# Edge stage of a two-layer graph network: twelve transposes in one run on TensorE, both message casts ahead of both relus on ScalarE

## The chip, the cores and the metric

The kernel runs on one core of one Trainium2 chip. The metric is the time of one execution in microseconds, the median of several runs. PE is TensorE's matmul path and PEld its weight load, DVE is VectorE, ACT is ScalarE, POOL is GpSimd, SP is SyncE.

## The reference

Two graph layers with residuals and layer norms over 6250 nodes of 256 features and 100000 edges sorted by destination. The change lies in the first layer:

```
src, dst = edge_index
ei   = concat([x[src], edge_attr], axis=-1)          # 256 + 64 features
core = maximum(ei @ W1 + b1, 0.0) @ W2 + b2
gate = sigmoid(ei @ Wg + bg)
msg  = gate * core
agg  = segment_sum(msg, dst, num_segments=N)
out  = layernorm(agg + x) * gamma + beta
x    = layernorm(x + out)
```

The second layer (two hops of a normalised sum over edges, a product, a log softmax) follows and is not touched.

## The kernel before, in words

Setup. `x @ [W1 | Wg]` plus biases is computed once for each node and stored as `p_table` (6250 rows of 512 numbers). The rows of one edge's source then bring in the node part of both products at once, and only the 64 edge features are left to multiply.

Edge stage. The edges are worked through in 196 groups of 512 (4 tiles of 128). Each engine has its own list of stages written out group by group; `at_group(stage, i, s, lag)` calls a stage for group G + lag in step G. Semaphores alone tie the engines together. For a group g:

- POOL, `gather` (L801): four indirect DMAs bring the rows of `p_table` into `gathered`, which has two places (g even or odd). It waits until `hidden_product` and `gate_seeded` of group g - 2 are done. Ahead of it POOL does `lower_msg` (L822) of the first half of the messages of group g - 4.
- ScalarE and VectorE split the edge features into an upper part and a remainder (`round_ea` L1285, `lower_ea` L1779). PE's `turn_ea` (L939) transposes them, four transposes into bank 7, and `copy_ea` (L1291) brings them back as `ea_turned_sb`, signalled by `ea_ready`.
- PE, `hidden_product`: for each of two banks k (0 and 1) the products of `w_e_hi` and `w_e_lo` with `ea_turned_sb`, 512 columns each (L950, L951), then four transposes of the gathered rows added on top (L953). Each bank has to be free first: `hidden_ready` of the group before.
- ScalarE, `upper_hidden(k)` (L1299): the relu of bank k into `hidden_hi`; VectorE, `lower_hidden(k)` (L1786): the remainder `hidden_lo`, which frees the bank.
- PE, `gate_product` (L963, L964): eight matmuls of 256 columns onto banks 2 and 3, which ScalarE has seeded with the gathered gate part (`seed_gate` L1329); `open_gate` (L1320) takes the sigmoid.
- PE, `core_product` (L976): 24 matmuls of 256 columns (three products of split factors for each of 4 tiles and 2 halves of the features) onto banks 4 and 5, seeded with the bias by `seed_core` (L1313).
- VectorE, `message` (L1796): gate times core for each half of the group, into `room`. ScalarE, `upper_msg(half)` (L1306): the upper part `msg_hi`. The remainder of half 0 is POOL's (L822), of half 1 VectorE's `lower_msg` (L1802).
- PE, `scatter` (L990, L992): eight matmuls of a one-hot matrix with both parts of the messages into bank 6. VectorE's `add_window` (L1828) adds the bank to `agg`; in a middle stretch of the stage once for two groups, else once for each group.

In step G, PE does the core product of G, the hidden and gate products of G + 2, the scatter of G - 1 and the edge features' transposes of G + 4, in this order. VectorE and ScalarE also work on finished chunks of 7 node blocks between their stages: VectorE in small pieces, ScalarE with the scaling of rows (L1336, L1343) and, once for each of the four EARLY chunks (EARLY = NC - 3), a cast of a whole chunk (L1383) just ahead of `copy_ea`.

Hops. After the edge stage come two hops over the graph and the last stage. They share no code with the change.

Of the kernel before, what the change touches and what calls it, by code (L numbers as in the profile page):

```python
# [8 lines left out]
P = 128  # L9
GROUP = 512  # L10
TILES = 4
# [39 lines left out]
def wait_count(engine, semaphore, count):  # L51

    if not isinstance(count, int) or count > 0:
        engine.wait_ge(semaphore, count)
# [131 lines left out]
def gnn_kernel(nc, x, src, dst, edge_attr, W1, b1, W2, b2, Wg, bg, gamma, beta, Wl, bl, out):  # L186
    N, H = x.shape
    E, DE = edge_attr.shape
    KC = H // P
# [35 lines left out]
    with ExitStack() as ctx:  # L225
        def sb(name, shape, dt=F32):
            return ctx.enter_context(nc.sbuf_tensor(name, shape, dt))

        def sem(name):
            return ctx.enter_context(nc.semaphore(name))  # L230

        banks = ctx.enter_context(nc.psum_tensor("banks", [P, 8, 512], F32))
# [5 lines left out]
        def at(name, offset, shape, dt=F32):  # L238

            return nc.alloc_sbuf_tensor_at(name, shape, dt, offset=arena_at + offset).ap()  # L240
# [4 lines left out]
        w_e_hi = at("w_e_hi", EDGE_AT, [P, H2], F32R)  # L245
        w_e_lo = at("w_e_lo", EDGE_AT + 2048, [P, H2], F32R)
# [5 lines left out]
        ea_turned_sb = at("ea_turned_sb", EDGE_AT + 14336, [P, 2, GROUP], F32R)  # L252
# [66 lines left out]
        ident = sb("ident", [P, P])  # L319
# [48 lines left out]
        gathered = sb("gathered", [P, 2, TILES, H2])  # L368
# [33 lines left out]
        S = {n: sem(n) for n in names}  # L402
# [23 lines left out]
        def over_groups(engine, step, first, last):  # L426

            for g in range(first, 2):
                step(g // 2, g % 2)
            with engine.Fori(1, R - 3) as i:  # L430
                for s in range(2):
                    step(i, s)
            for g in range(NG - 6, last):
                step(g // 2, g % 2)

        def msg_of(table, s, half):

            return table[:, TILES * s + 2 * half:TILES * s + 2 * half + 2, 0:H]

        def at_group(stage, i, s, lag):  # L440

            turn, slot = i + (s + lag) // 2, (s + lag) % 2
            if not isinstance(turn, int) or 0 <= 2 * turn + slot < NG:
                stage(turn, slot, 2 * turn + slot)
# [397 lines left out]
        def _(pe):  # L842
# [87 lines left out]
            for bank in range(2, 6):  # L930
                last = nc.tensor.matmul(banks[:, bank, :], ident[:, :], bias_in[:, :], start=True, stop=True)
# [8 lines left out]
                                               ea_split[:, s, j, :, :].bitcast(F32).rearrange("p b d -> p (b d)"), ident[:, :])  # L940
                last.then_inc(S["ea_turned"], 1)

            def hidden_product(turn, s, g):

                pe.wait_ge(S["ea_ready"], g + 1)
                pe.wait_ge(S[f"p_gathered{s}"], 16 * TILES * (turn + 1))
                for k in range(KC):
                    columns = slice(k * P, (k + 1) * P)
                    wait_count(pe, S["hidden_ready"], 2 * g + k - 1)
                    nc.tensor.matmul(banks[:, k, :], w_e_hi[:, columns], ea_turned_sb[:, s, :], start=True, stop=False)  # L950
                    nc.tensor.matmul(banks[:, k, :], w_e_lo[:, columns], ea_turned_sb[:, s, :], start=False, stop=False)  # L951
                    for j in range(TILES):
                        last = nc.tensor.matmul(banks[:, k, j * P:(j + 1) * P], gathered[:, s, j, columns], ident[:, :],  # L953
                                                start=False, stop=j == TILES - 1, is_transpose=True)
                    last.then_inc(S["hidden_product"], 1)

            def gate_product(turn, s, g):
# [56 lines left out]
            def edge_steps(scatter_stage, looped):  # L1014
                def step(i, s):
                    at_group(core_product, i, s, 0)
                    at_group(hidden_product, i, s, 2)
                    at_group(gate_product, i, s, 2)
                    at_group(scatter_stage, i, s, -1)
                    at_group(turn_ea, i, s, 4)  # L1020
                if looped:
                    over_groups(pe, step, -5, NG + 1)
                else:
                    for g in range(-5, NG + 1):
                        step(g // 2, g % 2)
# [217 lines left out]
        def _(act):  # L1243
# [49 lines left out]
            def upper_hidden(k):  # L1293

                def stage(turn, s, g):
                    if k == 0:
                        wait_count(act, S["core_done"], 2 * (g - 1))
                    act.wait_ge(S["hidden_product"], 2 * g + k + 1)
                    nc.scalar.activation(hidden_hi[s][k], banks[:, k, :], ACT.Relu).then_inc(S["hidden_upper"], 1)  # L1299
                return stage  # L1300

            def upper_msg(half):

                def stage(turn, s, g):
                    act.wait_ge(S["msg_ready"], 2 * g + half + 1)
                    nc.scalar.copy(msg_of(msg_hi, s, half), msg_of(msg, s, half)).then_inc(S["msg_upper"], 1)  # L1306
                return stage
# [46 lines left out]
            def node_rows_at(g):  # L1354

                for c in range(NC - 2):
                    j = g - begins[c + 1]
                    if 0 <= j < CHUNK:
                        normed_row(c, j)
                    if 1 <= j <= CHUNK:  # L1360
                        scaled_row(c, j - 1)

            def step(i, s, in_order=True):
                at_group(copy_ea, i, s, 3)
                at_group(round_ea, i, s, 5)
                if in_order and isinstance(i, int):
                    node_rows_at(2 * i + s)
                at_group(seed_gate, i, s, 2)
                at_group(upper_msg(0), i, s, 0)
                at_group(upper_hidden(0), i, s, 2)  # L1370
                at_group(upper_msg(1), i, s, 0)
                at_group(upper_hidden(1), i, s, 2)
                at_group(seed_core, i, s, 1)
                at_group(open_gate, i, s, 2)
# [110 lines left out]
            with act.If(in_order):  # L1485
                for g in range(-5, NG):
                    if g in upper_at:
                        upper_rows(upper_at.index(g))
                    step(g // 2, g % 2)
                upper_rows(EARLY)  # L1490
                for c in range(EARLY + 1, NC):
                    node_rows(c)
                    upper_rows(c)
                hops()
            with act.Else():
                over_groups(act, lambda i, s: step(i, s, False), -5, NG)
                act.wait_ge(S["agg_added"], NG)
                for c in range(NC):
                    node_rows(c)
                for c in range(NC):  # L1500
                    upper_rows(c)
                hops()
# [819 lines left out]
```

## Time and profile before

| | us |
|---|---|
| runs | 2490.89 (median), 2490.82, 2492.63 |
| profiled execution, span of the core | 2488.3 |
| PE busy in the span | 2315.5 |
| VectorE, ScalarE, POOL busy | 1927.1, 1651.3, 1641.2 |
| mean granted TensorE clock | 0.971 |

The profile is of one further execution. For it the profile gives the span, from its first to its last instruction, and no other time; the run times also hold what lies around the span. Lines of the order of time read: start in us from the span's start, duration in us, engine, line, operation, output and inputs, how many instructions were merged, and in brackets the engine's idle time before and what ended it. Matmul ends are modelled, so the next start may come before the end that is shown.

### The profile page before, as it was taken

What the parts mean: (1) busy time and instruction counts of PE and PEld (TensorE: products, weight loads), DVE (VectorE), ACT (ScalarE), POOL (GpSimd) and SP (SyncE); (2) the same over time, 40 slices, a digit from 0 to 9 for tenths busy, and PEclk for the clock granted to TensorE, in tenths of its full rate; (3) what the DMA queues carried; (4) which work ended last, traced back from release to release, by engine and by line L of the source; (5) the groups of instructions that cost most, each with busy time, mean ns of one, the idle gap of its engine ahead of it and who ended that gap; (6) DMA issues with size and microseconds to landing.
All of it is one profiled execution on the core that took longest, in us unless ns stands there. A gap on an engine that the chain in (4) does not pass through costs nothing. (4 is left out here: it accounts for less than half of the span.)

```text
span 2488.3 us, 48732 instructions
## 1 busy us (share of the span) xinstructions
PE 2315.5 (93%) x16053; PEld 1833.1 (74%) x16053; DVE 1927.1 (77%) x4467; ACT 1651.3 (66%) x3119; POOL 1641.2 (66%) x1581
## 2 busy tenths in 40 slices
PE   7889999999999999999999996689999999999973
PEld 3369999999999999999999995145555554555542
DVE  6748878888887877888888989998888874447673
ACT  1158888888888889889998996454577751013232
POOL 0177777777777777777777773355676763777773
PEclk9989999999999999999999998799999999999996
DMA  6465656655556556656666662345556635776652
GB/s 220 163 211 169 170 168 173 172 171 169 168 170 169 170 168 188 179 171 186 183 186 183 183 186 84 99 123 135 149 153 162 181 88 178 263 238 211 211 163 79
DMA packets 276158, 422.41 MB, mean 170 GB/s; under 512 B 127618, under 2 KB 198548, under 8 KB 273860
## 3 DMA queue, kind: packets, MB, share of 16 engines
q0 software_dynamic: 90368, 281.11, 39.3%
q1 hardware_dynamic: 170028, 116.99, 15.4%
q10 hardware_dynamic: 15512, 21.17, 2.5%
q8 instruction: 134, 2.20, 0.4%
q14 instruction: 116, 0.95, 0.1%
HBM read 354.78 MB, written 64.37 MB: 168 GB/s over the span
## 5 line engine op out<-in xcount | busy, mean ns | idle before, releaser
L801 POOL DMA_INDIRECT gathered<-p_table,src_t x784 | 773.4, 987 | 275.6 <-issue 196.8
L801 POOL DMA_INDIRECT gathered<-hop_table,src_t x576 | 584.0, 1014 | 336.0 <-issue 154.5
L976 PE MATMUL banks<-w_hi,hidden_hi 128*128 128x256 f32 x1568 | 458.3, 292 | 3.9 <-ACT banks L1313 3.8
L976 PE MATMUL banks<-w_lo,hidden_hi 128*128 128x256 f32 x1568 | 441.8, 282 | 0.0
L976 PE MATMUL banks<-w_hi,hidden_lo 128*128 128x256 f32 x1568 | 441.2, 281 | 0.0
L1426 ACT CAST counts<-banks 128x686 f32 (+3 forms) x382 | 295.8, 774 | 155.6 <-PE banks L1038 76.4
L1796 DVE TENSOR_TENSOR room<-banks,gate 128x512 f32<-128x512 f32 x392 | 265.3, 686 | 76.5 <-PE banks L976 75.8
L822 POOL TENSOR_TENSOR msg_lo<-room,msg_hi 128x512 fp32r<-128x512 f32 x196 | 250.7, 1279 | 93.4 <-ACT msg_hi L1306 92.3
L1299 ACT ACTIVATE hidden_hi<-banks 128x512 fp32r<-128x512 f32 x392 | 235.0, 600 | 114.2 <-PE banks L953 111.5
L976 PEld LDWEIGHTS banks<-w_hi,hidden_hi 128*128 128x128 f32 x1568 | 297.3, 190 | 5.9 <-issue 4.2
L976 PEld LDWEIGHTS banks<-w_lo,hidden_hi 128*128 128x128 f32 x1568 | 298.3, 190 | 0.0
L976 PEld LDWEIGHTS banks<-w_hi,hidden_lo 128*128 128x128 f32 x1568 | 297.6, 190 | 0.0
L1038 PE MATMUL banks<-codes,low_hot 128*128 128x343 f16 (+3 forms) x958 | 239.6, 332 | 57.9 <-DVE codes L2010 52.8
L1786 DVE SCALAR_TENSOR_TENSOR hidden_lo<-banks,hidden_hi 128x512 fp32r<-128x512 f32 x392 | 263.1, 684 | 37.7 <-ACT hidden_hi L1299 29.7
L1064 PE MATMUL banks<-parts,counts 128*128 128x512 f16 x980 | 286.7, 379 | 0.0
L1306 ACT CAST msg_hi<-room 128x512 fp32r<-128x512 f32 x392 | 242.5, 619 | 48.6 <-DVE room L1796 39.6
L1106 PE MATMUL banks<-gathered,hot_half 128*128 128x256 f16 x1152 | 221.7, 284 | 44.3 <-DMA gathered<-hop_table,src_t 40.0
L1106 PEld LDWEIGHTS banks<-gathered,hot_half 128*128 128x128 f16 x1152 | 113.8, 101 | 170.9 <-DMA gathered<-hop_table,src_t 48.7
L953 PE MATMUL banks<-ident,gathered 128*128 128x128 f32 x1568 | 235.5, 273 | 0.0
L953 PEld LDWEIGHTS banks<-ident,gathered 128*128 128x128 f32 x1568 | 196.5, 141 | 51.9 <-issue 0.4
L1329 ACT COPY banks<-gathered 128x512 f32<-128x512 f32 x392 | 223.8, 623 | 3.6 <-DMA gathered<-p_table,src_t 3.6
L2010 DVE TENSOR_SCALAR codes<-wide,code_c 128x686 f16<-128x686 f16 (+3 forms) x551 | 220.8, 401 | 0.0
(224 smaller groups left out, 5304.3 us busy)
## 6 DMA issues: line engine op xcount, KB each, us to landing
ea<-in_edge_attr SPq DMA_DIRECT2D x196, 128.0 KB
counts_saved<-counts SPq DMA_DIRECT2D x16, 1568.0 KB, 9.7
ring<-counts_saved SPq DMA_DIRECT2D x16, 1568.0 KB, 7.6
gathered<-p_table,src_t POOLq DMA_INDIRECT x784
p_table<-p_t ACTq DMA_DIRECT2D x48, 256.0 KB, 2.6
hop_table<-parts SPq DMA_DIRECT2D x12, 896.0 KB
gathered<-hop_table,src_t POOLq DMA_INDIRECT x576, 2.9
x_saved<-x_room SPq DMA_DIRECT2D x7, 896.0 KB, 6.1
```

What stands on the lines that cost most here:

```text
L801: pool.indirect_dma_start(out=rows[:, n % slots, j, :], out_offset=None, in_=table[:, :], in_offset=bass.IndirectOffsetOnAxis(ap=src_t[:, ...
L822: nc.gpsimd.tensor_tensor(msg_of(msg_lo, g % 2, 0), msg_of(msg, g % 2, 0), msg_of(msg_hi, g % 2, 0).bitcast(F32), ALU.subtract).then_inc(S ...
L953: last = nc.tensor.matmul(banks[:, k, j * P:(j + 1) * P], gathered[:, s, j, columns], ident[:, :], start=False, stop=j == TILES - 1, is_tr ...
L976: last = nc.tensor.matmul(banks[:, 4 + half, j % 2 * H:(j % 2 + 1) * H], lhs, rhs, start=False, stop=n == len(products) - 1, skip_group_ch ...
L1038: last = nc.tensor.matmul(banks[:, bank, 0:each], low[:, :], code[:, each * n:each * (n + 1)], start=opens, stop=closes and (n > 0 or not ...
L1064: last = nc.tensor.matmul(banks[:, 4 + m % 2, 0:H2], counts[:, b, P * (m % BLOCKS):P * (m % BLOCKS + 1)], parts[:, b, :], start=b == 0, st ...
L1106: last = nc.tensor.matmul(banks[:, bank_of_turn(k, turn), 0:H], hot_half[:, turn % HOT_TURNS * TILES + j, :], hop_rows[:, turn % HOP_SLOTS ...
L1299: nc.scalar.activation(hidden_hi[s][k], banks[:, k, :], ACT.Relu).then_inc(S["hidden_upper"], 1)
L1306: nc.scalar.copy(msg_of(msg_hi, s, half), msg_of(msg, s, half)).then_inc(S["msg_upper"], 1)
L1426: nc.scalar.copy(in_blocks_of(e, coming.pop(0) + shared, width - shared), product_of(e, int(shared))).then_inc(S["evac_done"], 1)
L1786: nc.vector.scalar_tensor_tensor(out=hidden_lo[s][k], in0=banks[:, k, :], scalar=0.0, in1=hidden_hi[s][k].bitcast(F32), op0=ALU.max, op1=A ...
L1796: nc.vector.tensor_tensor(msg_of(msg, s, half), banks[:, 4 + half, :].rearrange("p (j n) -> p j n", j=2), gate[s][:, 2 * half:2 * half + 2 ...
```

## The change

On PE the eight transposes of the gathered rows leave `hidden_product` and become a stage of their own, `turn_rows`, which opens both banks. In the step, `turn_ea` moves from the end to behind the core product, with `turn_rows` behind it. The 512-column products are then added onto the transposed rows. On ScalarE `upper_msg(1)` moves ahead of `upper_hidden(0)`.

```diff
-            def hidden_product(turn, s, g):
-
-                pe.wait_ge(S["ea_ready"], g + 1)
+            def turn_rows(turn, s, g):
+
                 pe.wait_ge(S[f"p_gathered{s}"], 16 * TILES * (turn + 1))
                 for k in range(KC):
                     columns = slice(k * P, (k + 1) * P)
                     wait_count(pe, S["hidden_ready"], 2 * g + k - 1)
-                    nc.tensor.matmul(banks[:, k, :], w_e_hi[:, columns], ea_turned_sb[:, s, :], start=True, stop=False)
-                    nc.tensor.matmul(banks[:, k, :], w_e_lo[:, columns], ea_turned_sb[:, s, :], start=False, stop=False)
                     for j in range(TILES):
-                        last = nc.tensor.matmul(banks[:, k, j * P:(j + 1) * P], gathered[:, s, j, columns], ident[:, :],
-                                                start=False, stop=j == TILES - 1, is_transpose=True)
+                        nc.tensor.matmul(banks[:, k, j * P:(j + 1) * P], gathered[:, s, j, columns], ident[:, :],
+                                         start=j == 0, stop=False, is_transpose=True, skip_group_check=True)
+
+            def hidden_product(turn, s, g):
+
+                pe.wait_ge(S["ea_ready"], g + 1)
+                for k in range(KC):
+                    columns = slice(k * P, (k + 1) * P)
+                    nc.tensor.matmul(banks[:, k, :], w_e_hi[:, columns], ea_turned_sb[:, s, :], start=False, stop=False,
+                                     skip_group_check=True)
+                    last = nc.tensor.matmul(banks[:, k, :], w_e_lo[:, columns], ea_turned_sb[:, s, :], start=False, stop=True,
+                                            skip_group_check=True)
                     last.then_inc(S["hidden_product"], 1)
...
             def edge_steps(scatter_stage, looped):
                 def step(i, s):
                     at_group(core_product, i, s, 0)
+                    at_group(turn_ea, i, s, 4)
+                    at_group(turn_rows, i, s, 2)
                     at_group(hidden_product, i, s, 2)
                     at_group(gate_product, i, s, 2)
                     at_group(scatter_stage, i, s, -1)
-                    at_group(turn_ea, i, s, 4)
...
                 at_group(seed_gate, i, s, 2)
                 at_group(upper_msg(0), i, s, 0)
+                at_group(upper_msg(1), i, s, 0)
                 at_group(upper_hidden(0), i, s, 2)
-                at_group(upper_msg(1), i, s, 0)
                 at_group(upper_hidden(1), i, s, 2)
```

The order on PE from the last matmul of a core product to the first of the gate product, before. L950 and L951 are the 512-column products, L953 the transposes of gathered rows:

```order
L976 MATMUL banks<-w_hi,hidden_lo_66 128x256
L950 MATMUL banks<-ea_turned_sb,w_e_hi 128x512 [waits hidden_ready,p_gathered0,ea_ready]
L951 MATMUL banks<-ea_turned_sb,w_e_lo 128x512
L953 MATMUL banks<-ident,gathered 128x128 x4
L950 MATMUL banks<-ea_turned_sb,w_e_hi 128x512 [waits hidden_ready]
L951 MATMUL banks<-ea_turned_sb,w_e_lo 128x512
L953 MATMUL banks<-ident,gathered 128x128 x4
L963 MATMUL banks<-w_e_hi,ea_turned_sb 128x256 [waits gate_seeded]
```

A third run of four transposes (L939) stands at the end of the step, ahead of the next core product.

The same place after the change. L983 is the core product, L950 now the transposes of gathered rows, L958 and L960 the 512-column products:

```order
L983 MATMUL banks<-w_hi,hidden_lo_66 128x256
L939 MATMUL banks<-ident,ea_split 128x128 [waits ea_ready,ea_split]
L939 MATMUL banks<-ident,ea_split 128x128 x3
L950 MATMUL banks<-ident,gathered 128x128 [waits hidden_ready,p_gathered0]
L950 MATMUL banks<-ident,gathered 128x128 x3
L950 MATMUL banks<-ident,gathered 128x128 [waits hidden_ready]
L950 MATMUL banks<-ident,gathered 128x128 x3
L958 MATMUL banks<-ea_turned_sb,w_e_hi 128x512 [waits ea_ready]
L960 MATMUL banks<-ea_turned_sb,w_e_lo 128x512
L958 MATMUL banks<-ea_turned_sb,w_e_hi 128x512
L960 MATMUL banks<-ea_turned_sb,w_e_lo 128x512
L970 MATMUL banks<-w_e_hi,ea_turned_sb 128x256 [waits gate_seeded]
```

All twelve transposes of a step now stand between the core product and the first 512-column product, and the next core product follows the scatter.

The order on ScalarE from the gate's seeding to the gate's sigmoid, before:

```order
L1329 COPY banks<-gathered 128x512 [waits gate_ready]
L1306 CAST msg_hi<-room 128x2x256 [waits msg_ready]
L1299 ACTIVATE hidden_hi_63<-banks 128x512 [waits hidden_product,core_done]
L1306 CAST msg_hi<-room 128x2x256 [waits msg_ready]
L1299 ACTIVATE hidden_hi_64<-banks 128x512 [waits hidden_product]
L1313 COPY banks<-bias_core 128x512 [waits msg_ready] x2
L1320 ACTIVATE gate_59<-banks 128x512 [waits msg_ready,gate_product] x2
```

And after the change:

```order
L1337 COPY banks<-gathered 128x512 [waits gate_ready]
L1314 CAST msg_hi<-room 128x2x256 [waits msg_ready] x2
L1307 ACTIVATE hidden_hi_61<-banks 128x512 [waits hidden_product,core_done]
L1307 ACTIVATE hidden_hi_62<-banks 128x512 [waits hidden_product]
L1321 COPY banks<-bias_core 128x512 [waits msg_ready] x2
```

The second cast of the messages (L1306, now L1314) went from between the relus (L1299, now L1307) to ahead of both.

## Rows read from the trace of the kernel before

**Rows 1.** The page: span, and busy time of each engine.

```profile
span 2488.3 us, 48732 instructions
...
PE 2315.5 (93%) x16053; PEld 1833.1 (74%) x16053; DVE 1927.1 (77%) x4467; ACT 1651.3 (66%) x3119; POOL 1641.2 (66%) x1581
```

**Rows 2.** Windows, first to last core product: length, busy (count) by engine, PEclk, DMA.

```profile
163.75:1529.54 1365.79, 1362.30 (x10881) 1309.51 (x10881) 1136.00 (x2081) 1206.18 (x2405) 1010.07 (x967) 1.00 0.61 174
```

**Rows 3.** Waits of PE in the edge stage: us in total, times, longest.

```profile
PE banks L976 <- ACT banks L1313: 3.8, 6, 1.2
```

**Rows 4.** Order of time on PE in one group.

```profile
600.03 0.40 PE L950 MATMUL banks<-ea_turned_sb,w_e_hi 128*128 128x512 f32 x1
...
600.50 0.60 PE L953 MATMUL banks<-ident,gathered 128*128 128x128 f32 x4
...
600.83 0.27 PE L953 MATMUL banks<-ident,gathered 128*128 128x128 f32 x1
600.85 0.48 PE L950 MATMUL banks<-ea_turned_sb,w_e_hi 128*128 128x512 f32 x1
601.17 0.39 PE L951 MATMUL banks<-ea_turned_sb,w_e_lo 128*128 128x512 f32 x1
601.40 0.60 PE L953 MATMUL banks<-ident,gathered 128*128 128x128 f32 x4
...
603.61 0.28 PE L992 MATMUL banks<-msg_lo,hot_window 128*128 128x256 f32 x1
...
604.09 0.36 PE L976 MATMUL banks<-w_hi,hidden_hi 128*128 128x256 f32 x1
```

**Rows 5.** Groups by line and form, edge stage, PE: busy us, mean ns, idle before.

```profile
L950 PE MATMUL banks<-ea_turned_sb,w_e_hi 128*128 128x512 f32 x388 | 169.0, 435 | 0.0
L951 PE MATMUL banks<-ea_turned_sb,w_e_lo 128*128 128x512 f32 x388 | 152.7, 393 | 0.0
```

**Rows 6.** Order of time on PE in the setup, transposes of L852 and L907.

```profile
45.76 0.38 PE L852 MATMUL banks<-ident,agg 128*128 128x128 f32 x2
45.98 0.60 PE L907 MATMUL banks<-ident,gathered 128*128 128x128 f32 x4
46.41 1.88 PE L860 MATMUL banks<-room,x_turned_sb 128*128 128x512 f32 x4
```

**Rows 7.** Order of time on ScalarE in the same group as rows 4.

```profile
601.19 0.60 ACT L1299 ACTIVATE hidden_hi<-banks 128x512 fp32r<-128x512 f32 x1 [0.90 <-PE banks L953]
...
602.69 1.11 ACT L1313 COPY banks<-bias_core 128x512 f32<-128x512 f32 x2
...
604.69 0.60 ACT L1291 CAST ea_turned_sb<-banks 128x512 fp32r<-128x512 f32 x1
```

**Rows 8.** Order of time in a group that waits, on ScalarE and PE.

```profile
1017.67 1.72 ACT L1383 ACTIVATE parts<-agg 128x1792 f16<-128x1792 f32 x1
...
1023.67 1.11 ACT L1313 COPY banks<-bias_core 128x512 f32<-128x512 f32 x2
...
1024.42 0.36 PE L976 MATMUL banks<-w_hi,hidden_hi 128*128 128x256 f32 x1
```

**Rows 9.** Order of time on VectorE in the same group as rows 4.

```profile
600.23 0.69 DVE L1796 TENSOR_TENSOR room<-banks,gate 128x512 f32<-128x512 f32 x1 [0.59 <-PE banks L976]
...
604.06 0.48 DVE L1828 SCALAR_TENSOR_TENSOR agg<-banks,first_row,agg 128x257 f32 x1 [0.54 <-PE banks L992]
...
605.97 0.68 DVE L1796 TENSOR_TENSOR room<-banks,gate 128x512 f32<-128x512 f32 x1
```

**Rows 10.** Order of time on POOL in the same group as rows 4.

```profile
602.27 0.96 POOL L801 DMA_INDIRECT gathered<-p_table,src_t  x1 [0.70 <-PE banks L953]
```

**Rows 11.** Setup and start of the edge stage: windows view, and PE in order of time.

```profile
29.00:41.00 12.00, 12.00 (x66) 7.75 (x65) 7.14 (x12) 1.49 (x4) 0.00 (x0) 1.00 0.71 256
...
150.00:158.00 8.00, 4.47 (x17) 3.91 (x18) 1.17 (x3) 2.81 (x7) 4.28 (x6) 0.50 0.78 244
...
154.52 1.05 PE L953 MATMUL banks<-ident,gathered 128*128 128x128 f32 x4
```

## Prediction

> **What bounds the kernel now.** I read the page first, then the windows view over the edge stage, then the order of time on each engine inside one group. The page says a span of 2488.3 us in which PE is busy 93% and nothing else over 77% [rows 1]. The change touches only the edge stage. Its 196 groups of 512 edges run from the first core product at 163.75 to the last at 1529.54: 1365.79 us for 195 steps, 7.00 us each, with PE busy 1362.30 of it at a clock of 1.00 [rows 2]. PE's waits in this stage are one line, 3.8 us in 6 waits [rows 3]. So the stage costs what PE's instruction stream costs. Another order on ScalarE can give back at most these 3.8 us; all else must come out of PE's own spacing. In the order of time on PE the reader should look at the starts, since ends are modelled: 512-column matmuls start 0.23 us apart, and a run of four transposes stands between the others three times in a group [rows 4].
>
> **PE: twelve transposes in one run.** No instruction is added or removed: per group still 12 transposes, 4 matmuls of 512 columns and 40 of 256 or 258. What changes is how often a run of transposes ends: three times before, once after.
> A tempting row is the first matmul behind a run: L950 at 600.85 shows 0.48 us, where L951 shows 0.39 [rows 4]. Over the stage L950 has a mean of 435 ns against L951's 393; only every second L950 stands behind a run, so that is 84 ns a run [rows 5]. Taken as a fee for the switch, two switches fewer would save 2 x 0.084 x 196 = 33 us.
> I don't take it so. Count from start to start: the first run begins at 600.50, the second matmul behind it at 601.17. Take off one 512-column matmul (0.23, 601.17 to 601.40): four transposes cost 0.44, 0.11 each [rows 4]. The matmul behind the run is booked as started only 0.02 us after the last transpose (600.83 and 600.85) and pays the rest of that transpose's 0.11 inside its own longer row. The 84 ns are the missing part of the last transpose, not something on top of it. A longer run in the setup says the same: six transposes from 45.76 to 46.41, 0.65 us, again 0.11 each [rows 6]. A run of n costs n x 0.11 from start to start, whatever n is; twelve in one run cost what 3 x 4 do. By the rows a transpose streams 128 columns and still takes nearly as long as a product of 256, (7.00 - 12 x 0.11 - 4 x 0.23)/40 = 0.12; what both have in common is a new load of weights ahead of each.
> The Trainium skill has the reason, in "TensorE: Matmul & The Clock Gate", section "LDWEIGHTS (loading the stationary operand)": a load takes its columns over 1.2 in ns, 107 ns for 128 columns, whatever the matmuls around it are. By that rule twelve transposes take 12 x 107 ns in one run or in three, and nothing is saved; with the 84 ns as a fee it would be 33 us. It speaks against a gain here.
> Bounds: the rows are good to 0.01 us, so two ends of a run fewer are worth between 0 and 2 x 0.01 x 196 = 3.9 us. I take **-1 us**, since 0.44 for a run is nearer to 4 x 0.11 than to anything 0.01 above it.
>
> **PE's new order, and who waits.** Let 0 be the end of the core product, where L950 starts (600.03). Before, the first relu starts at 601.19, +1.16, 0.09 after the modelled end of its bank's last transpose (600.83 and four in 0.60 from 600.50, 601.10) [rows 4, 7]. In the change the 12 transposes take 1.31, the two 512-column matmuls of the first bank start at +1.31 and +1.54, and the second ends at 1.54 + 0.39 = +1.93, so the relu can start at +2.02. The second bank is ready 0.46 later. ScalarE's instructions follow each other in 0.50 (relu, cast, relu from 601.19 to 602.69), so the second relu starts at about +2.52 and seed_core at +3.02, where it stood at +2.66 [rows 7]. What does PE need? In a group that waits, seed_core started at 1023.67 and the core product at 1024.42, 0.75 later [rows 8]. The next core product is due at 604.09, +4.06 [rows 4], so seed_core may start as late as +3.31. Margin 0.65 before, **0.29 after**: no wait in a plain group. ScalarE also has the room, busy 1206.18/195 = 6.19 of 7.00 us [rows 2]. The rest, edit by edit:
> - turn_ea now stands right behind the core product. Its ea_ready comes from L1291, which starts at 604.69 and takes 0.60; 0.36 later it ends at 605.65 and is wanted at 607.03. Margin 1.4 [rows 7].
> - upper_msg(1) ahead of upper_hidden(0): its message starts at 600.23, +0.20, and takes 0.69, so the cast runs from about +0.96 to +1.58, in time in which ScalarE stood idle (0.90 before the relu) [rows 7, 9]. It costs nothing; it would be paid in full if the message came 0.45 later.
> - The scatter now closes the group: its last matmul moves from 603.61, +3.58, to about +4.01. VectorE's add_window started 0.45 after it and starts 0.43 later; behind it stand lower_msg, lower_ea and the first message, which goes from 605.97 to 606.40 and ends at 607.1. The second message is due at 607.23 [rows 4, 9]. Hidden, with 0.1 to spare; late next is that second message, wherever node work lies between.
> - POOL: the gather waits for hidden_product, and starts at 602.7 in place of 602.27 [rows 10]; lower_msg also moves back by 0.4. POOL is busy 1010.07/195 = 5.2 of 7.00 us [rows 2], the loop closes, and the rows land 0.4 later, for a product two groups on.
> - turn_rows waits for hidden_ready of the group before; VectorE's hidden_lo of it is done half a group earlier. Nothing.
>
> **Groups that wait.** PE's 3.8 us of waits lie in few groups [rows 3]. In four (one for each of the EARLY chunks) ScalarE has a 1.72 us cast of node rows, and everything behind it is late; there seed_core, not PE, sets the step [rows 8]. In some others VectorE's node work does it. After, two things are added there: the second cast must wait for a message that comes 0.6 behind the first, where ScalarE would go on after 0.5, +0.10; and ScalarE enters the group 0.36 later. In the four that is 4 x 0.46 = 1.8 us. In the others 0.1 to 0.5 each, 1 us together. In the last thirty groups a window is added in every group, not every second, and VectorE has no room for the 0.43: a few new waits, 0 to 2 us, I take 0.5. Together **+3.3 us**, bounds 0 (ScalarE's unbroken pairs take it all back) and +8 (twice as many groups wait).
>
> **Sum.** -1 + 3.3 = +2.3 us on the profiled span of 2488.3. The median of the three runs is 2490.89, 2.6 above that span, which is what lies around it; so 2490.9 + 2.3 = **2493 us**.
>
> **Rivals.**
> A. The 84 ns are a real fee. For: the longer rows [rows 4, 5]. Against: start-to-start times and the run of six [rows 4, 6]. Time: 2490.9 - 33 + 2.3 = 2460. Chance 0.07.
> B. ScalarE's chain becomes the bound, and it is slower: hidden_product, relu, relu, seed_core, core product, in every group. It decides when the first relu starts more than 0.29 us behind my +2.02. For: the margin halves, and no row of before shows a relu behind a 512-column matmul. Against: the relu's 0.09 behind the modelled end, and ScalarE's 6.19 of 7.00. With the relu 0.35 late it is 0.06 x 190 = 11 us, 2504; with 0.5 late 40 us, 2533. Chance 0.12, half of it near the lower figure.
> C. The clock. Twelve transposes in a row are 1.3 us with few columns streamed. If the granted clock fell to 1.2 GHz in that stretch, the row at a clock of 0.50 prices it: four transposes 1.05 us against 0.60 [rows 4, 11]; 12 would lose 1.35 us a group, 265 us in all, 2755. Against: a stretch of 12 us in the setup in which runs of 10 and 18 transposes alternate with four products each holds 1.00 [rows 11]. Chance 0.02.
> D. The reordering works and the new waits don't come: 2490, inside the forecast's range. That it does not do what it says is excluded: in the order one run of twelve stands in place of three, and both casts ahead of the relus.
>
> **How the numbers follow.** Forecast 0.79, A 0.07, B 0.12, C 0.02. A measurement of this kernel tells about 0.2% from no change, 5 us: the band is 2485.9 to 2495.9. The forecast's own bounds are 2490.9 - 3.9 = 2487 and 2490.9 + 8 = 2499; what lies above the band is 0.05 of chance. Slower: 0.05 + 0.11 of B + 0.02 = 0.18. Faster: A and a hundredth beside it, 0.08. Same: 0.74. The range is 2487 to 2501: A, C and the dearer part of B are left out, the cheapest part of B is in.
>
> **What would show it.** Twelve transposes starting 0.11 apart, then 512-column matmuls from +1.31; plain steps of 6.99 to 7.00 us; the first relu at +2.0 and seed_core at +3.0; PE waiting 5 to 8 us in all for seed_core in place of 3.8; the clock at 1.00 throughout. I am wrong if a plain step is 6.84 (A), if it is over 7.02 with PE waiting for seed_core in every group (B), or if another wait (ea_ready, hidden_ready) shows there.

## The result, and the profile after

The changed kernel takes 2495.36 us (median of 14 runs, 2493.0 to 2497.92), the kernel before 2490.32 us beside it (14 runs, 2488.6 to 2494.08). The ratio is 1.002, with a 95% interval of 1.0012 to 1.0027: 5 us slower, just at the 0.2% that the prediction named as the edge of what can be told. The forecast was 2493 in a range of 2487 to 2501. The profiled execution has a span of 2492.8 us, 4.5 more than before.

The page of the changed kernel, span and busy time by engine, against [rows 1]:

```profile
span 2492.8 us, 48731 instructions
...
PE 2315.2 (93%) x16053; PEld 1851.6 (74%) x16053; DVE 1941.9 (78%) x4467; ACT 1665.5 (67%) x3119; POOL 1629.8 (65%) x1581
```

PE's work is the same. VectorE and ScalarE show 15 and 14 us more for the same instructions; of VectorE's, 14 us lie in one instruction (the one-hot, L1809 before and L1817 now, a mean of 1.12 us before and 1.20 after), of which the last section tells.

The windows view from the first to the last core product, against [rows 2], with the same columns:

```profile
164.79:1534.50 1369.71, 1363.98 (x10880) 1327.96 (x10881) 1150.12 (x2081) 1220.78 (x2405) 1000.60 (x966) 1.00 0.60 173
```

The stage takes 1369.71 us, 3.92 more. What comes behind it takes 958.3 us in place of 958.8. The clock is 1.00 as before, so rival C is out for the stage.

The waits of PE in that stage, against [rows 3]:

```profile
PE banks L983 <- ACT banks L1321: 5.0, 7, 1.3
PE banks L939 <- ACT ea_turned_sb L1299: 0.7, 4, 0.2
```

The first line is seed_core, 5.0 in place of 3.8 us. The second is new: turn_ea waits for the edge features' copy in four groups.

The order of time on PE in one group, from the end of the core product to the first gate matmul, against [rows 4]:

```profile
601.51 0.28 PE L983 MATMUL banks<-w_hi,hidden_lo 128*128 128x256 f32 x1
601.63 0.60 PE L939 MATMUL banks<-ident,ea_split 128*128 128x128 f32 x4
602.07 1.04 PE L950 MATMUL banks<-ident,gathered 128*128 128x128 f32 x8
602.86 0.48 PE L958 MATMUL banks<-ea_turned_sb,w_e_hi 128*128 128x512 f32 x1
603.17 0.39 PE L960 MATMUL banks<-ea_turned_sb,w_e_lo 128*128 128x512 f32 x1
603.40 0.40 PE L958 MATMUL banks<-ea_turned_sb,w_e_hi 128*128 128x512 f32 x1
603.64 0.39 PE L960 MATMUL banks<-ea_turned_sb,w_e_lo 128*128 128x512 f32 x1
603.87 0.28 PE L970 MATMUL banks<-w_e_hi,ea_turned_sb 128*128 128x256 f32 x1
```

From 601.63 to 603.17, less one 512-column matmul of 0.23, the twelve transposes take 1.31 us, 12 x 0.109. Only behind the last transpose is there a long 512-column row, 0.48. The other long rows are gone, and nothing was won by it: where a matmul was booked 0.02 us behind the last transpose of a run, the next transpose now starts a full 0.11 behind it.

ScalarE in the same group, against [rows 7]:

```profile
601.63 0.62 ACT L1314 CAST msg_hi<-room 128x512 fp32r<-128x512 f32 x1
602.56 0.62 ACT L1314 CAST msg_hi<-room 128x512 fp32r<-128x512 f32 x1 [0.31 <-DVE room L1804]
603.66 1.09 ACT L1307 ACTIVATE hidden_hi<-banks 128x512 fp32r<-128x512 f32 x2 [0.49 <-PE banks L960]
604.64 1.11 ACT L1321 COPY banks<-bias_core 128x512 f32<-128x512 f32 x2
```

With 601.63 as 0 the relus start at +2.03 and seed_core at +3.01; the prediction had +2.02 and +3.02. VectorE's add_window (606.10) is at +4.47, predicted +4.46.

The plain step is read best over 100 groups. Before, and after the change, starts of core products:

```profile
303.09 0.36 PE L976 MATMUL banks<-w_hi,hidden_hi 128*128 128x256 f32 x1
...
1003.09 0.36 PE L976 MATMUL banks<-w_hi,hidden_hi 128*128 128x256 f32 x1
```

```profile
304.63 0.28 PE L983 MATMUL banks<-w_hi,hidden_hi 128*128 128x256 f32 x1
...
1004.96 0.28 PE L983 MATMUL banks<-w_hi,hidden_hi 128*128 128x256 f32 x1
```

100 steps take 700.00 us before and 700.33 after: 3 ns a step more, 0.6 us over the stage.

The start-up, on PE, before: idle times over 0.2 us from the first transposes of edge features to the first core product.

```profile
146.45 1.12 PE L939 MATMUL banks<-ident,ea_split 128*128 128x128 f32 x4 [4.34 <-DVE ea_split L1779]
148.33 1.09 PE L939 MATMUL banks<-ident,ea_split 128*128 128x128 f32 x4 [0.77 <-ACT ea_turned_sb L1291]
153.53 0.77 PE L950 MATMUL banks<-ea_turned_sb,w_e_hi 128*128 128x512 f32 x1 [4.11 <-DMA gathered<-p_table,src_t]
...
163.75 0.36 PE L976 MATMUL banks<-w_hi,hidden_hi 128*128 128x256 f32 x1 [0.42 <-ACT banks L1313]
```

And after:

```profile
145.19 1.12 PE L939 MATMUL banks<-ident,ea_split 128*128 128x128 f32 x4 [4.61 <-DVE ea_split L1787]
...
152.13 1.97 PE L950 MATMUL banks<-ident,gathered 128*128 128x128 f32 x8 [2.12 <-DMA gathered<-p_table,src_t]
159.47 0.73 PE L939 MATMUL banks<-ident,ea_split 128*128 128x128 f32 x4 [2.37 <-ACT ea_turned_sb L1299]
164.79 0.36 PE L983 MATMUL banks<-w_hi,hidden_hi 128*128 128x256 f32 x1 [0.32 <-ACT banks L1321]
```

From the first transposes to the first core product it was 163.75 - 146.45 = 17.30 us and is now 164.79 - 145.19 = 19.60, 2.3 us more. PE stands 2.37 us at turn_ea, waiting for ScalarE's copy, with eight transposes and the hidden product of another group behind it in the queue. Before, turn_ea was the last stage of a step and nothing was behind it but the next step. ScalarE starts that copy only at 158.73, behind this step's relus (which wait for PE's hidden product), a table load of 1.28 us and the sigmoids.

The wait is only part of the loss. While PE stood there the granted clock was 1.00 (157 to 159 us); once it went on it fell to 0.50, that is 1.2 GHz (160 to 163.1 us). The windows view from turn_ea to the first gate matmul, with the columns of [rows 2]:

```profile
159.47:163.36 3.89, 3.89 (x17) 3.56 (x17) 0.42 (x1) 1.72 (x4) 1.12 (x2) 0.56 0.73 222
```

The same twelve transposes and four products take 603.87 - 601.63 = 2.24 us in the plain group shown above. Against that, the slow clock costs 1.65 us here. The kernel before works at 0.50 up to 159 us and at 1.00 from 160 us on; the changed one was at 1.00 by 157 us and lost it again. How the 2.3 us divide between wait and clock, these two profiles don't tell.

In this profile the setup ahead of the first transposes was 1.3 us shorter, which hides half of the loss. The granted clock goes with it: between 105 and 115 us it is 1.00 in the profile of the changed kernel and 0.83 in the one before. It stays at 1.00 in the profiles of five of the six kernels here that have turn_ea moved forward, and in none of the eight others; but e8 and f8 are the same kernel and have 0.83 and 1.00. Whether this is chance is open.

The long steps: in the group with the first whole-chunk cast, against [rows 8], after the change:

```profile
1019.83 1.72 ACT L1391 ACTIVATE parts<-agg 128x1792 f16<-128x1792 f32 x1
...
1022.16 0.63 PE L939 MATMUL banks<-ident,ea_split 128*128 128x128 f32 x4 [0.17 <-ACT ea_turned_sb L1299]
...
1025.90 1.11 ACT L1321 COPY banks<-bias_core 128x512 f32<-128x512 f32 x2
...
1026.64 0.36 PE L983 MATMUL banks<-w_hi,hidden_hi 128*128 128x256 f32 x1
```

That step takes 7.68 us (7.33 before). The four steps with a cast are 7.68, 7.61, 7.61, 7.37 (before 7.33, 7.26, 7.26, 7.00). From the start of the cast to seed_core it is 6.07 us, before 6.00; the rest of the 0.35 is that ScalarE enters the group later. Over all steps longer than 7.035 us, the first two left out, the excess above 7.00 sums to 6.0 us, before to 3.1.

So, of the profiled pair: start-up +2.3, long steps +2.9, plain steps +0.6, less 1.3 ahead of the stage and 0.5 behind it; the first two steps (13.78 us, before 13.33) make up the rest to 4.5. The runs tell which parts are real.

### The profile page after: what moved, and what is told of

Same layout as the page of the kernel before. It is cut to its first block and busy times, and to the rows that moved or that the text cites. A ratio compares the mean times of both kernels' runs of the same rounds, so it can differ in the third digit from the quotient of the medians.

```text
span 2492.8 us, 48731 instructions
## 1 busy us (share of the span) xinstructions
PE 2315.2 (93%) x16053; PEld 1851.6 (74%) x16053; DVE 1941.9 (78%) x4467; ACT 1665.5 (67%) x3119; POOL 1629.8 (65%) x1581
## 5 line engine op out<-in xcount | busy, mean ns | idle before, releaser
L801 POOL DMA_INDIRECT gathered<-p_table,src_t x784 | 762.4, 972 | 284.2 <-issue 193.8
L983 PE MATMUL banks<-w_hi,hidden_hi 128*128 128x256 f32 x1568 | 442.8, 282 | 5.4 <-ACT banks L1321 5.0
L983 PE MATMUL banks<-w_lo,hidden_hi 128*128 128x256 f32 x1568 | 442.8, 282 | 0.0
L983 PE MATMUL banks<-w_hi,hidden_lo 128*128 128x256 f32 x1568 | 442.1, 282 | 0.0
L1794 DVE SCALAR_TENSOR_TENSOR hidden_lo<-banks,hidden_hi 128x512 fp32r<-128x512 f32 x392 | 252.2, 684 | 86.9 <-ACT hidden_hi L1307 85.6
L822 POOL TENSOR_TENSOR msg_lo<-room,msg_hi 128x512 fp32r<-128x512 f32 x196 | 252.3, 1287 | 98.0 <-ACT msg_hi L1314 97.4
L983 PEld LDWEIGHTS banks<-w_hi,hidden_hi 128*128 128x128 f32 x1568 | 297.2, 190 | 7.4 <-issue 3.6
L983 PEld LDWEIGHTS banks<-w_hi,hidden_lo 128*128 128x128 f32 x1568 | 298.5, 190 | 0.0
L983 PEld LDWEIGHTS banks<-w_lo,hidden_hi 128*128 128x128 f32 x1568 | 297.5, 190 | 0.0
L1314 ACT CAST msg_hi<-room 128x512 fp32r<-128x512 f32 x392 | 240.2, 625 | 80.6 <-DVE room L1804 71.8
L1307 ACT ACTIVATE hidden_hi<-banks 128x512 fp32r<-128x512 f32 x392 | 213.2, 596 | 75.2 <-PE banks L960 74.1
L1817 DVE TENSOR_TENSOR hot_window<-iota,lo_t 128x512 fp32r<-128x512 f32 x196 | 234.3, 1195 | 0.0
L1321 ACT COPY banks<-bias_core 128x512 f32<-128x512 f32 x392 | 218.4, 601 | 0.0
```

The lines of the kernel that those rows point to most:

```text
L801: pool.indirect_dma_start(out=rows[:, n % slots, j, :], out_offset=None, in_=table[:, :], in_offset=bass.IndirectOffsetOnAxis(ap=src_t[:, ...
L822: nc.gpsimd.tensor_tensor(msg_of(msg_lo, g % 2, 0), msg_of(msg, g % 2, 0), msg_of(msg_hi, g % 2, 0).bitcast(F32), ALU.subtract).then_inc(S ...
L983: last = nc.tensor.matmul(banks[:, 4 + half, j % 2 * H:(j % 2 + 1) * H], lhs, rhs, start=False, stop=n == len(products) - 1, skip_group_ch ...
L1794: nc.vector.scalar_tensor_tensor(out=hidden_lo[s][k], in0=banks[:, k, :], scalar=0.0, in1=hidden_hi[s][k].bitcast(F32), op0=ALU.max, op1=A ...
L1817: nc.vector.tensor_tensor(hot_window[:, TILES * s:TILES * (s + 1), :], iota[:, :].unsqueeze(1).to_broadcast([P, TILES, P]), columns.unsque ...
```

## The experiments

Twelve runs in four sets, each compared with the kernel before on the same chip.

**e1_pe_only.** TensorE's part alone.

```diff
                 at_group(upper_msg(0), i, s, 0)
-                at_group(upper_msg(1), i, s, 0)
                 at_group(upper_hidden(0), i, s, 2)
+                at_group(upper_msg(1), i, s, 0)
                 at_group(upper_hidden(1), i, s, 2)
```

(against the changed kernel)

> TensorE's part of the change alone, ScalarE's order as before (the second message cast stands between the relus again). My theory (weight loads set the pace of the transposes, and what PE loses it loses to late seeds): the first relu starts at +1.97 as in the change, the cast and the second relu follow in steps of 0.50, so seed_core starts at about +3.44, 0.13 behind the +3.31 that PE needs. A plain step is 7.10 to 7.14 us and the kernel takes 2515 to 2525 us. Rival (ScalarE's reordering is what costs the 5 us, PE's part is free): 2490 to 2492 us, plain step 7.00.

Measured: 2534.68 us, ratio 1.0177 (1.0161 to 1.0192). ScalarE and PE, in order of time:

```profile
601.52 0.60 ACT L1307 ACTIVATE hidden_hi<-banks 128x512 fp32r<-128x512 f32 x1 [1.04 <-PE banks L960]
602.01 0.61 ACT L1314 CAST msg_hi<-room 128x512 fp32r<-128x512 f32 x1
602.52 0.60 ACT L1307 ACTIVATE hidden_hi<-banks 128x512 fp32r<-128x512 f32 x1
603.01 1.11 ACT L1321 COPY banks<-bias_core 128x512 f32<-128x512 f32 x2
...
603.75 0.35 PE L983 MATMUL banks<-w_hi,hidden_hi 128*128 128x256 f32 x1
```

seed_core is at 603.01, the core product 0.74 later, and the plain step is 7.21 us. The rival (ScalarE's order is what costs) is out; without ScalarE's part TensorE's costs 44 us. My figure was low: it added the 0.50 of one cast to a seed_core at +2.94, where the changed kernel's stands at +3.01. The relu at +2.03 and three intervals of together 1.49 give +3.52, 0.21 behind the prediction's limit of +3.31, and 0.21 x 195 = 41 of the 44 us. It is rival B of the prediction, made real by one cast of 0.5 us (the prediction had priced a delay of 0.5 at 40 us), and it shows that the margin was in truth 0.3 us.

**e2_act_only.** ScalarE's part alone, on the kernel before (the same two lines, the other way).

> ScalarE's part alone, TensorE's order as before. My theory: both banks' relus have room, seed_core starts 0.05 to 0.1 earlier, PE's plain step stays 7.00 and the waits stay 3 to 5 us in all: 2489 to 2492 us. Rival (the second cast ahead of the first relu delays the chain by itself): 2494 to 2496 us, as in the change.

Measured: 2491.32 us, ratio 1.0 (0.9991 to 1.0009). ScalarE's order costs nothing by itself and brings nothing by itself: PE waits for seed_core 4.5 us in the profile, plain step 7.00. In the trace, though, two of the long steps, the one three groups behind the first cast and the last but two, are 7.86 and 7.72 us as in the changed kernel (7.87 and 7.69; before 7.63 and 7.37). So about 0.6 of the changed kernel's 2.9 us in long steps come from ScalarE's order alone.

**e3_ea_last.** The whole change, with turn_ea left at the end of the step.

```diff
                     at_group(core_product, i, s, 0)
-                    at_group(turn_ea, i, s, 4)
                     at_group(turn_rows, i, s, 2)
...
                     at_group(scatter_stage, i, s, -1)
+                    at_group(turn_ea, i, s, 4)
```

> The whole change except that turn_ea stays at the end of the step: eight transposes in one run behind the core product, four ahead of the next. My theory: the wait of turn_ea for ea_ready goes, the relus come 0.44 earlier (first at +1.53), seed_core at about +2.5, and the long steps shrink to those of before: 2489 to 2492 us, plain step 7.00. Rival A (a fee of 0.084 us for each run of transposes left): one run more than in the change would make it 16 us slower than the change, 2511 us. Rival 2 (opening the banks with transposes costs PE something): 2494 to 2496 us.

Measured: 2492.62 us, ratio 1.0008 (0.9999 to 1.0017). The start-up is back at 17.0 us:

```profile
148.89 1.12 PE L939 MATMUL banks<-ident,ea_split 128*128 128x128 f32 x4 [4.34 <-DVE ea_split L1787]
...
155.76 1.97 PE L950 MATMUL banks<-ident,gathered 128*128 128x128 f32 x8 [3.90 <-DMA gathered<-p_table,src_t]
165.90 0.36 PE L983 MATMUL banks<-w_hi,hidden_hi 128*128 128x256 f32 x1 [0.41 <-ACT banks L1321]
```

In the stage no wait for ea_turned_sb is left, the first two steps take 13.27 us (13.33 before), and the steps with the first three casts are 7.33, 7.31 and 7.31 in place of 7.68, 7.61 and 7.61. The profile has one odd step of 7.72, where PE waited 0.49 us for gathered rows. With one run of transposes more than the changed kernel it is not 16 us slower but 3 us faster. The 0.6 us past my upper figure of 2492 is a plain step that alternates between 6.99 and 7.02; why it does I did not try to find.

**e5_more_runs.** The kernel before with the same twelve transposes in eight runs in place of three.

```diff
                     nc.tensor.matmul(banks[:, k, :], w_e_hi[:, columns], ea_turned_sb[:, s, :], start=True, stop=False)
-                    nc.tensor.matmul(banks[:, k, :], w_e_lo[:, columns], ea_turned_sb[:, s, :], start=False, stop=False)
                     for j in range(TILES):
+                        if j == 2:
+                            nc.tensor.matmul(banks[:, k, :], w_e_lo[:, columns], ea_turned_sb[:, s, :], start=False, stop=False)
...
+                    if g + 5 < NG:
+                        turn_one(g + 5, j)
...
-                    at_group(turn_ea, i, s, 4)
+                    if looped or 2 * i + s < 1:
+                        at_group(turn_ea, i, s, 4)
```

(turn_one is one of turn_ea's four transposes, behind each tile of the scatter)

> The kernel before, with the same twelve transposes of a group in eight runs in place of three: 2 + 2 in each of the two banks around the second 512-column matmul, and the four of the edge features one by one between the scatter's matmuls. Theory (a transpose costs its own or the next weight load, 0.109 us, wherever it stands): plain step 7.00 to 7.02 us, 2489 to 2494 us. Rival A (leaving a run costs 0.084 us): 5 x 0.084 x 196 = 82 us more, 2572 us, plain step 7.42.

Measured: 2494.2 us, ratio 1.0013 (1.0004 to 1.0023); the plain step is 7.026 us, both just above what my theory had. The scatter with single transposes between, on PE:

```profile
604.69 0.28 PE L1003 MATMUL banks<-msg_lo,hot_window 128*128 128x256 f32 x1
604.81 0.27 PE L939 MATMUL banks<-ident,ea_split 128*128 128x128 f32 x1
604.84 0.36 PE L1001 MATMUL banks<-msg_hi,hot_window 128*128 128x258 f32 x1
605.04 0.28 PE L1003 MATMUL banks<-msg_lo,hot_window 128*128 128x256 f32 x1
605.16 0.27 PE L939 MATMUL banks<-ident,ea_split 128*128 128x128 f32 x1
```

Each lone transpose has its long row behind it (0.36 against 0.28) and yet costs 0.11: from 604.81 to 605.16 are a transpose and two matmuls, 0.35 = 0.11 + 2 x 0.12. Five more runs cost 0.026 us a step, 5 ns each, where a fee of 84 ns would have made 0.42 us and 82 us in all. Rival A is out. The reason, that the next load of weights sets the pace, agrees with all of this, and no run varied the load alone.

**e4_cast_spread, e8_rows_first, e9_both_cures, e6_before_spread.** These four ran together, on a chip where the kernel before took 2648.76 us.

> The whole change, and the four casts of a chunk of node rows (1.72 us each on ScalarE, ahead of copy_ea) cut into pieces of two blocks, one piece a group, ahead of the relus. Theory (about half of the 5 us is four groups in which the cast makes everything late, 0.6 us each after the change against 0.3 before): the long steps at the casts go, PE's waits for seed_core fall, 2492.5 to 2494 us, start-up as in the change. Rival (the cost is in every plain group, or in noise of the start): 2495 to 2497 us.

> The whole change with turn_rows ahead of turn_ea in the run of twelve. Theory (in the start-up PE waits 2.4 us at turn_ea for ea_ready, with eight transposes behind it that it could have done): from the first transposes to the first core product 19.6 us become 17.9 to 18.7, the rest stays, 2494 to 2495 us. Rival (the start-up is only the gather's chance from run to run): 19.6 us stays or varies with no relation to the order, 2495 to 2496 us.

> The whole change with turn_ea back at the end of the step and the four casts cut into pieces. Theory (the loss is start-up plus late groups, and nothing is in the transposes' order itself): 2490 to 2492 us, no difference from the kernel before that can be told; start-up 17.0 to 17.4 us; no step over 7.3 us in the middle of the stage. Rival (opening the banks with transposes costs by itself): 2493 us or more.

> The kernel before with the four casts cut into pieces, nothing else. Theory: the three or four steps of 7.3 us go, 1 us in all, 2489 to 2491 us, which can hardly be told from before. Rival (the pieces delay more groups than the whole cast did, since each costs its own start): 2492 us or more.

Measured: e4 2716.37 us (ratio 1.0258, 1.0231 to 1.0286), e8 2689.87 (1.0155, 1.0127 to 1.0182), e9 2681.9 (1.0128, 1.0099 to 1.0156), e6 2677.39 (1.0102, 1.007 to 1.0134). None of these answers its question. On this chip VectorE and ScalarE stop together for about 2 us in many groups, while PE and POOL go on, as here in e6 (VectorE, then ScalarE):

```profile
477.12 0.68 DVE L1811 TENSOR_TENSOR room<-banks,gate 128x512 f32<-128x512 f32 x1
479.95 0.69 DVE L1811 TENSOR_TENSOR room<-banks,gate 128x512 f32<-128x512 f32 x1 [2.15 <-remote]
```

```profile
477.84 0.62 ACT L1306 CAST msg_hi<-room 128x512 fp32r<-128x512 f32 x1
480.09 0.60 ACT L1299 ACTIVATE hidden_hi<-banks 128x512 fp32r<-128x512 f32 x1 [1.63 <-PE banks L953]
```

The profile names no cause within the core. All that can be read is that the change's order with turn_ea in front (e8) loses 1.5% there and 0.2% elsewhere; that it is the smaller margin that tells is a guess. Three of the four had a fault of mine besides: the edit moved VectorE's work on the chunk by two groups as well (`lower_at = [g + 4 ...]`), SP's store of the chunk waited for it, and the loads of edge features stood behind the store. In e6 ScalarE waited for them in 6 places:

```profile
ACT ea_split L1285 <- DMA ea<-in_edge_attr: 35.2, 6, 8.6
```

The four were run again on other chips, with the fault removed.

**f8_rows_first.** The whole change, turn_rows ahead of turn_ea.

```diff
                     at_group(core_product, i, s, 0)
-                    at_group(turn_ea, i, s, 4)
                     at_group(turn_rows, i, s, 2)
+                    at_group(turn_ea, i, s, 4)
                     at_group(hidden_product, i, s, 2)
```

> The same kernel as e8 again (the whole change with turn_rows ahead of turn_ea), on another chip, since the chip of the second call ran the kernel before in 2649 us. Theory as there: start-up from the first transposes to the first core product 17.9 to 18.7 us in place of 19.6, time 2494 to 2495 us. Rival: 19.6 us, 2495 to 2496 us.

Measured: 2494.72 us, ratio 1.0021 (1.0012 to 1.003). The start-up is 163.58 - 145.59 = 17.99 us, and the wait for the copy 1.58 us in place of 2.37:

```profile
145.59 1.12 PE L939 MATMUL banks<-ident,ea_split 128*128 128x128 f32 x4 [4.56 <-DVE ea_split L1787]
...
160.73 0.63 PE L939 MATMUL banks<-ident,ea_split 128*128 128x128 f32 x4 [1.58 <-ACT ea_turned_sb L1299]
163.58 0.36 PE L983 MATMUL banks<-w_hi,hidden_hi 128*128 128x256 f32 x1 [0.35 <-ACT banks L1321]
```

The trace shows the start-up cured by 1.6 us. Most of it is the clock. PE stood 1.58 us in place of 2.37, and from there to the first core product the granted clock is 1.00:

```profile
160.73:163.58 2.85, 2.50 (x17) 2.15 (x17) 1.52 (x3) 2.85 (x7) 2.06 (x3) 1.00 0.73 214
```

The changed kernel takes 164.79 - 159.47 = 5.32 us from the end of its wait to the core product: of the 2.47 us more, 1.65 are the slow clock and the other 0.82 the eight transposes that f8 has ahead of the wait. The copy itself came 0.8 us later, counted from the first gathered rows. No run varied PE's idle time alone. The first two steps take 13.78 us as in the changed kernel; moving turn_ea behind turn_rows does not cure them. Nor does it change the cast groups: there PE no longer waits for the copy, and the four steps are still 7.68, 7.61, 7.61 and 7.35. In the time the cure can't be seen: the interval covers both readings, so this rests on the trace alone. The stage itself (1369.77 us) is that of the change.

**f4_cast_pieces.** The whole change, each of the four casts in four pieces over two groups.

```diff
+                if known:
+                    piece_at(2 * i + s, 0)
                 at_group(upper_msg(1), i, s, 0)
+                if known:
+                    piece_at(2 * i + s, 1)
                 at_group(upper_hidden(0), i, s, 2)
...
-                    if g in upper_at:
-                        upper_rows(upper_at.index(g))
```

(piece_at casts two blocks of the chunk, in the two groups from upper_at on)

> The whole change with each of the four whole-chunk casts cut into four pieces over two groups, one ahead of each of the places where ScalarE is idle, and VectorE's part and the stores left at their old groups (in e4 they had moved by two groups, and the edge features' loads queued behind the stores). Theory: the four steps of 7.6 us go, 2492.5 to 2494 us; ScalarE never waits over 2 us for the edge features. Rival (the long steps come from VectorE's node work alone): 2495 to 2496 us, steps of 7.6 stay.

Measured: 2494.42 us, ratio 1.0014 (1.0005 to 1.0023). The step at the first cast went from 7.68 to 7.05, with one of 7.33 behind it, and the others from 7.61, 7.61 and 7.37 to at most 7.19. But the step of 7.87 three groups behind the first cast grew to 8.19; there ScalarE waits 2.44 us for a message that stands behind VectorE's node work. The stage is 1.26 us shorter, half of what I expected.

**f9_both_cures.** The whole change with e3's and f4's edits.

> The whole change with turn_ea back at the end of the step and the four casts in pieces over two groups (as f4). Theory (the loss is start-up plus late groups; nothing is in opening the banks with transposes): 2490 to 2492 us, the interval of the ratio reaches 1.000; start-up 17.0 to 17.4 us. Rival (something else of TensorE's order costs too): 2493 us or more.

Measured: 2491.79 us, ratio 1.0009 (1.0 to 1.0018). Start-up 162.92 - 145.74 = 17.2 us, stage 1366.88 us, within 1.1 us of before. With turn_ea at the end and the casts in pieces, most of the 5 us is back though both banks are still opened by transposes. What may be left, some 2 us, is too small for these runs.

**f6_before_pieces.** The kernel before with f4's pieces, both ahead of the first relu.

> The kernel before with the four casts in pieces over two groups. Theory: the three steps of 7.3 us at the casts go, 0.8 us; 2489 to 2491 us, hardly to be told from before. Rival (pieces cost more than they free): 2492 us or more.

Measured: 2490.3 us, ratio 0.9999 (0.999 to 1.0008). The stage is 1365.22 us in the trace, 0.6 shorter: the steps at the casts are gone, but the step of 7.63 grew to 8.20. No version was found that beats the kernel before.

## Why the prediction was right, and where it was not

- **What bounds the stage.** Right. PE's stream sets 7.00 us a step, and e1 shows the other regime: as soon as ScalarE's chain is behind, the step follows it.
- **The twelve transposes.** Right in the point that mattered: the 84 ns behind a run are the last transpose's own time. The merged run took 12 x 0.109, and e5's eight runs cost 5 ns a run more, not 84. The size of the term was off by sign: -1 us predicted, +0.6 measured (3 ns a step). By e5's 5 ns two ends fewer should have brought 2 us over the stage; other spacings ate them, which at 0.01 us in a row can't be assigned.
- **The margin of 0.29 us.** Right: +2.03 and +3.01 against +2.02 and +3.02, and e1 confirms both the threshold and the 0.75 us between seed_core and the core product.
- **Groups that wait.** Predicted +3.3, measured +2.9. The four casts cost +0.35, +0.35, +0.35 and +0.37, 1.4 us in place of 1.8, and the steps right behind them 0.3 together. f8 shows that this is seed_core's lateness, as predicted, and not turn_ea's new wait: with that wait gone from these groups the steps are the same.
- **The term that was missing: turn_ea's new wait.** I gave it a "Margin 1.4" from a plain group and left it there; the sum had no term for it. In the start-up ScalarE is not that far ahead: PE stands 2.37 us at turn_ea, as nothing can pass it in PE's queue, and then runs the next 3 us at a clock of 0.50. Together that is 2.3 us up to the first core product and 0.45 us in the first two steps. e3 takes all of it away; f8 takes away 1.6 us, mostly the slow clock. In four cast groups PE also waits there, 0.7 us in all, which f8 shows to cost nothing. The prediction had named another wait (ea_ready) as a sign that it is wrong, and by its own sign this part of it is.
- **The sum.** +2.3 predicted, +5.0 measured (1.0012 to 1.0027, which is 3.0 to 6.7 us). In the traces the terms are +0.6 for the transposes, +2.9 for groups that wait and +2.75 for the start with its first two steps, 6.2 together; the setup and what follows the stage take 1.8 of it back in the profiled pair. So the sum missed 2.75 us at the start and 1.6 us in the transposes' term, and that the time still lay near the forecast is in part luck. "Same" was given 0.74; the measured ratio lies on the edge between it and slower.
- **Rivals.** A is out by e3 and e5, C by the clock of 1.00 in the stage; the clock did fall in the start-up, but behind a wait. B did not come about, but e1 shows that it was one 0.5 us cast away.

## What to carry to other kernels

A longer row behind an instruction can be that instruction's own time booked late: count from start to start over the whole run before calling it a fee. When a stage with a wait is moved forward in an engine's queue, ask what stands behind it not only in a plain step but in the first ones, where the engines are not yet in phase; and look at the granted clock behind the wait, which was most of the 1.6 us that f8 won back. An edit that brings nothing alone can be what another one needs: here ScalarE's order is worth nothing alone and 39 us beside TensorE's.

## What the runs showed beside this

VectorE's one-hot (L1817) and POOL's subtraction (L822) block each other, and the first to start is served. In e1 VectorE starts first; its row is 0.68 us, and POOL's is 1.52:

```profile
607.49 0.68 DVE L1817 TENSOR_TENSOR hot_window<-iota,lo_t 128x512 fp32r<-128x512 f32 x1
```

```profile
607.71 1.52 POOL L822 TENSOR_TENSOR msg_lo<-room,msg_hi 128x512 fp32r<-128x512 f32 x1 [0.51 <-ACT msg_hi L1314]
```

In the changed kernel POOL starts first, with 1.19, and VectorE's row is 1.63:

```profile
602.33 1.19 POOL L822 TENSOR_TENSOR msg_lo<-room,msg_hi 128x512 fp32r<-128x512 f32 x1 [0.32 <-ACT msg_hi L1314]
```

```profile
602.44 1.63 DVE L1817 TENSOR_TENSOR hot_window<-iota,lo_t 128x512 fp32r<-128x512 f32 x1
```

The Trainium skill states it in "SBUF — State Buffer", section "Who interferes with whom": a VectorE instruction with two SBUF inputs contends with a GpSimd instruction that reads SBUF, and issue order decides who blocks. Both traces agree. The prediction moved POOL's subtraction by 0.4 us and did not ask what it would now meet; VectorE had the room in a plain group.
